# Post-norm attention and FFN layer on eight cores: WQ folds moved between the K/V chunks, and LayerNorm 1 moved into the attention loop

## The reference

```python
Q = x @ WQ.T + bQ                       # 2048 -> 16 heads of 128
K = (x @ WK.T + bK)  # 4 groups of 128  -> tiled 4 times to 2048 columns
V = (x @ WV.T + bV)  # the same
scores = einsum('btd,bsd->bts', Q, K)   # one score matrix over all 2048 columns
scores = where(causal, -inf, scores)
attn = softmax(scores) / sqrt(128)
x = layernorm(x + einsum('bts,bsd->btd', attn, V) @ proj)      # LayerNorm 1
g = (x @ gate_w.T) * gate_s ; u = (x @ up_w.T) * up_s
x = layernorm(x + ((silu(g) * u) @ down_w.T) * down_s)         # LayerNorm 2
```

## Time and profile before

| | us |
|---|---|
| median of two runs | 2189.18 (2187.82 to 2190.53) |
| the profiled execution | 2190.91 |
| its span on the slowest core (core 5) | 2189.3 |
| spans of the eight cores | 2161.7 to 2189.3 |
| TensorE busy | 1559.2 (71% of the span) |
| VectorE busy | 369.8 (17%) |
| ScalarE busy | 158.3 (7%) |
| gate and up matmuls (L698, L708) | 319.7 + 318.3 |
| down matmuls (L780) | 309.8 |

### The profile page before, as it was taken

How to read it: one execution, slowest core, us unless ns; L and a number is a source line. 1 busy time by engine, 2 the same in 40 slices (tenths; PEclk the granted TensorE clock), 3 DMA queues, 4 the chain that set the end, 5 groups by cost and what they waited for, 6 DMA issues and landing times. The chain is left out here.

```text
span 2189.3 us, 19673 instructions; the slowest of 8 cores (2161.7 to 2189.3 us)
## 1 busy us (share of the span) xinstructions
PE 1559.2 (71%) x7922; PEld 783.3 (36%) x7922; DVE 369.8 (17%) x510; ACT 158.3 (7%) x169; POOL 149.7 (7%) x143
## 2 busy tenths in 40 slices
PE   3269999645655556462009999999999969999930
PEld 0024443211212112120004444444444438888830
DVE  0000000014132232411600111111111110000035
ACT  1000000001000010100301111111111000000011
POOL 1100000010000000000001111111111100000000
PEclk9999999856565665655559999999999979999965
DMA  6955531370030300205495777777777784674466
GB/s 92 137 81 77 77 58 19 78 124 0 0 115 0 115 0 30 86 0 172 193 194 60 75 76 76 76 75 76 76 76 76 77 111 83 96 118 83 80 213 259
DMA packets 298527, 192.25 MB, mean 88 GB/s; under 512 B 201946, under 2 KB 284099, under 8 KB 291269
## 3 DMA queue, kind: packets, MB, share of 16 engines
q0 software_dynamic: 258240, 106.97, 41.4%
q1 hardware_dynamic: 40198, 84.02, 11.7%
HBM read 255.98 MB, written 37.75 MB: 134 GB/s over the span
## 5 line engine op out<-in xcount | busy, mean ns | idle before, releaser
L698 PE MATMUL gups<-x1T,gstr 128*128 128x512 bf16 x1408 | 319.7, 380 | 138.1 <-DMA x1T<-x1bd 138.1
L708 PE MATMUL gups<-x1T,ustr 128*128 128x512 bf16 x1408 | 318.3, 379 | 0.0
L780 PE MATMUL dnps<-dstr,hT 128*128 128x256 bf16 x2816 | 309.8, 274 | 10.3 <-DMA dstr<-dTd 10.3
L780 PEld LDWEIGHTS dnps<-dstr,hT 128*128 128x128 bf16 x2816 | 276.5, 98 | 45.0 <-issue 11.9
L698 PEld LDWEIGHTS gups<-x1T,gstr 128*128 128x128 bf16 x1408 | 138.1, 98 | 306.0 <-issue 140.9
L708 PEld LDWEIGHTS gups<-x1T,ustr 128*128 128x128 bf16 x1408 | 137.7, 98 | 166.2
L519 PE MATMUL zpn<-vv,aT_sb 128*128 128x512 bf16 x256 | 129.5, 609 | 79.4 <-DVE aT_sb L512 79.4
L723 DVE SCALAR_TENSOR_TENSOR hT<-gups,us_col,silu 128x512 bf16<-128x512 f32 x88 | 66.1, 751 | 592.4 <-PE gups L708 592.4
L314 PE MATMUL kps<-xch,wk_sb 128*128 128x512 bf16 x512 | 120.5, 390 | 44.2 <-DMA xch<-xT 42.0
L687 POOL DMA_DIRECT2D gstr<-gTd x44 | 50.3, 1144 | 1149.0 <-DMA x1bd<-x1s 625.1
L454 PE MATMUL scps<-kT,qsT 128*128 128x512 bf16 x256 | 78.7, 466 | 70.4 <-DVE scores L463 65.8
(11 more groups left out here) (96 smaller groups left out, 676.0 us busy)
## 6 DMA issues: line engine op xcount, KB each, us to landing
gstr<-gTd POOLq DMA_DIRECT2D x44, 512.0 KB, 7.7
ustr<-uTd POOLq DMA_DIRECT2D x44, 512.0 KB, 9.5
dstr<-dTd POOLq DMA_DIRECT2D x8, 2816.0 KB, 20.9
xch<-xT POOLq DMA_DIRECT2D x8, 2048.0 KB, 16.5
wq4b<-wq POOLq DMA_DIRECT2D x16, 512.0 KB, 6.5
masks<-msk SPq DMA_DIRECT2D x8, 1024.0 KB, 7.9
pjt<-prj POOLq DMA_DIRECT2D x16, 512.0 KB, 5.6
xqp<-xq SPq DMA_DIRECT2D x32, 256.0 KB, 5.9
```

The source lines that it names most:

```text
L698: (lambda bi, tch, gsl, ct: lambda e: e.matmul(gups[:, gsl, :], gstr[bi][:, ct, :], x1T[:, ct, tch*512:(tch+1)*512], start=(ct == 0), stop ...
L708: (lambda bi, tch, usl, ct: lambda e: e.matmul(gups[:, usl, :], ustr[bi][:, ct, :], x1T[:, ct, tch*512:(tch+1)*512], start=(ct == 0), stop ...
L780: (lambda bi, ts, ps, it: lambda e: e.matmul(dnps[ps][:, 0:256], hT[:, it, ts*128:(ts+1)*128], dstr[bi][:, it, :], start=(it == 0), stop=( ...
```

## The change

Three things are changed. The debug outputs are removed as well, which were not built.

First, in A1, the loads of the first x chunk, wk, the second x chunk and wv are issued first. The folds become a function, `plan_wq_fold`, that is called four times after the V product of each of the first four chunks. It accumulates in `kps` bank 0 instead of `vps` bank 0.

Second, in B, the body of the loop becomes three functions: `plan_scores`, `plan_z` (P times V with its transposes) and `plan_proj_ln1`. The projection of a group is planned after the scores of the next group and before its P times V. `plan_proj_ln1` also does LayerNorm 1 of each q tile in place, right after its four column blocks, and stores x1. Stage C, its DRAM tensor `y1d` and one barrier are gone. To make room, the proj rows are loaded into `Pq` instead of `pjtile`.

Third, the reciprocal root in both LayerNorms is Exp(-0.5 * Ln(var)) on ScalarE, instead of Sqrt on ScalarE and a reciprocal on VectorE.

```diff
+                    mx_pre[0] = B.dma("gpsimd",
...
+                                      "sxc0", [("pe", mp_a0), ("ve", mv_a0)])
+                    m_wk = B.dma("gpsimd", lambda e: e.dma_start(out=wk_sb[:], in_=wk_r),
+                                 "swkv")
+                    mx_pre[1] = B.dma("gpsimd",
...
+                                      "sxc1")
+                    m_wv = B.dma("gpsimd", lambda e: e.dma_start(out=wv_sb[:], in_=wv_r),
+                                 "swkv")
...
+                    def plan_wq_fold():
+                        dt_ = fold_dt[0]
+                        fold_dt[0] += 1
+                        fbi = dt_ % 2
+                        swq = "swq%d" % fbi
+                        mwq = B.dma("gpsimd",
...
+                                    swq, [("pe", wqf_free[fbi])])
+                        nonlocal_mk = mk_kfree_ref[0]
+                        for r in range(4):
+                            B.op("tensor",
+                                 (lambda fbi, r: lambda e: e.matmul(
+                                     kps[:, 0, :], idb_sb[:], wq4buf[fbi][:, r, :],
+                                     start=(r == 0), stop=(r == 3)))(fbi, r),
+                                 [(swq, mwq), ("ve", mv_a0), ("se", nonlocal_mk)]
+                                 if r == 0 else (),
...
+                        wqf_free[fbi] = B.m("pe")
+                        B.op("scalar",
...
+                        mk_kfree_ref[0] = B.m("se")
...
                     for pi, rc in enumerate(proc):
...
+                        if pi in mx_pre:
+                            mx = mx_pre[pi]
+                        else:
+                            mx = B.dma("gpsimd",
...
+                        if pi < 4:
+                            for _ in range(4):
+                                plan_wq_fold()
...
-                                 [("pe", mp_pj), (sxq, mxq), (sy, y1st[tq])],
+                                 [("pe", mp_pj), (sxq, mxq), (sx, slot_st[tq])],
...
+                        B.op("vector",
+                             (lambda q, tq: lambda e: e.tensor_reduce(
+                                 l1s[:, q:q+1], y1s[:, tq, :], axis=AX.X, op=OP.add))(q, tq),
+                             (), [("ve", 1)])
+                        B.op("scalar",
+                             (lambda q, tq: lambda e: e.activation(
+                                 out=sqscr[:], in_=y1s[:, tq, :], func=AF.Square,
+                                 accum_out=l1q[:, q:q+1]))(q, tq),
...
+                                 out=l1t[:, q:q+1], in_=l1v[:, q:q+1], func=AF.Ln))(q),
+                             [("ve", mv_var)], [("se", 1)])
...
+                                 out=l1r[:, q:q+1], in_=l1t[:, q:q+1], func=AF.Exp,
+                                 scale=-0.5))(q),
...
+                                 out=y1s[:, tq, :], in0=y1s[:, tq, :],
+                                 scalar1=l1nm[:, q:q+1], scalar2=l1r[:, q:q+1],
...
+                                 y1s16[:, tq, :], y1s[:, tq, :]))(tq),
...
+                                  out=x1f_r[q], in_=y1s[:, tq, :]))(q, tq),
+                              sx, [("ve", mv_a)])
...
+                                  out=x1b_r[q], in_=y1s16[:, tq, :]))(q, tq),
+                              sx)
+                        slot_st[tq] = B.m(sx)
...
+                pending = None
+                for g in range(4):
+                    plan_scores(g)
+                    if pending is not None:
+                        plan_proj_ln1(pending)
+                    plan_z(g)
+                    pending = g
+                plan_proj_ln1(pending)
```

More of the change, by code:

```diff
@@ L247, in build_program @@
                     B.begin()
-                    mvid = mv_a0
+                    proc = [2, 3, 4, 5, 6, 7, 0, 1]
+                    xuse = [0, 0]
+                    mk_kfree = 0
+                    mk_vfree = 0
                     wqf_free = [0, 0]
[L250 to L266, removed]
-                        wqf_free[bi] = B.m("pe")
-                        B.op("scalar",
-                             (lambda dt_: lambda e: e.activation(
-                                 out=wqsT[:, dt_, :], in_=vps[:, 0, :],
-                                 func=AF.Copy))(dt_),
-                             [("pe", wqf_free[bi])], [("se", 1)])
-                        mk_kfree = B.m("se")
@@ L438, in build_program, with plan_scores @@
                 pj_free = [mv_fold, mv_fold]
-                y1st = [0, 0]
                 xq_free = [0, 0]
                 zevac = 0
-                for g in range(4):
+                slot_st = [0, 0]
+                zT_used = 0
+                def plan_scores(g):
+                    nonlocal exp_prev
                     for q in (2 * g, 2 * g + 1):
@@ L534, in build_program @@
                                      zn_sb[:, tq, dv*128:(dv+1)*128], idb_sb[:]))(tq, dv),
[L535 removed]
+                                 [("ve", mv_zn), ("pe", zT_used)] if dv == 0 else (),
                                  [("pe", 1)] if dv == 3 else ())
@@ new lines, in plan_proj_ln1 @@
+                        B.op("vector",
+                             (lambda q: lambda e: e.tensor_scalar(
+                                 out=l1v[:, q:q+1], in0=l1v[:, q:q+1],
+                                 scalar1=float(EPS), scalar2=None, op0=OP.add))(q),
+                             (), [("ve", 1)])
+                        mv_var = B.m("ve")
+                        B.op("scalar",
+                             (lambda q: lambda e: e.activation(
+                                 out=l1t[:, q:q+1], in_=l1v[:, q:q+1], func=AF.Ln))(q),
+                             [("ve", mv_var)], [("se", 1)])
@@ L857, in build_program @@
             B.op("scalar", lambda e: e.activation(
-                out=tmp8[:], in_=var8[:], func=AF.Sqrt),
+                out=tmp8[:], in_=var8[:], func=AF.Ln),
                 [("ve", mv_v)], [("se", 1)])
+            B.op("scalar", lambda e: e.activation(
+                out=rstd8[:], in_=tmp8[:], func=AF.Exp, scale=-0.5),
+                (), [("se", 1)])
             ms_v = B.m("se")
-            B.op("vector", lambda e: e.reciprocal(rstd8[:], tmp8[:]),
-                 [("se", ms_v)], [("ve", 1)])
-            mv_r = B.m("ve")
             o_free = [0, 0]
```

207 lines of the change are left out of this document (82 added, 125 removed).

## The result

The changed kernel takes 2204.12 us (median of 18 runs), the kernel before 2196.37 us beside it (16 runs): a ratio of 1.0045, 95% interval 1.0032 to 1.0059. It is slower by 0.45%, far inside the 2% that I called no change; I had predicted 2197 us, within 2165 to 2232. That forecast stood on 2189.2 us for the kernel before, so it was 8 us more; 0.45% is 10 us more. The profiled execution's slowest core is core 3.

The account below looks back on a forecast made before the run. TensorE was taken as starved in the first 129 us and the 94 us between attention and FFN. Sum: 2190.9 + 39 (stage A) - 32 (B and C) = 2198, predicted as 2197 us, range 2165 to 2232.

Parts of the forecast that it names:

- the loads do not hide (1): Rival in A1: the x loads hide, all four fold blocks last 13.4 us, 35 us less, 2162; chance 0.15.
- not in 33 (2): Rival in A1: x chunk lands after 32.5 us, sharing engines with fold loads; 36 us more, 2233; chance 0.10.
- one in each stage with activations (3): Rival in LayerNorm: Ln and Exp need two table loads in each of eight, 20.5 us, 2217; chance 0.05.
- no step of P times V passes the LayerNorm (4): Rival in attention: P times V steps proceed while LayerNorm waits, saving up to 54 us, 2143; chance 0.03.
- (1): Start of A1: x, wk and wv loaded first, in at about 69 us (64 to 74), 60 us earlier.
- (2): A1, folds between chunks: two run at once, two wait for loads; next K starts at 13.4 us.
- (3): A1, GpSimd queue: x chunk waits behind fold loads at three places, 25 us each (20.8 to 29); blocks total 88.4.
- (4): A1: four more K rows start after waiting at the lower clock, 4 x 2.7 = 11.0 us, at least 0.
- A1 in sum: Stage A total: -60 + 88.4 + 11.0 = +39 us, between +15 and +56.
- (5): Attention, VectorE: P times V copies stand behind projection and LayerNorm 1 of two tiles, 42.5 us (38 to 48).
- (6): Attention: a pair takes 142.8 us; x1 transposes start at 1080.0 instead of 1111.9, gain 32 us (10 to 50).
- (7): Stage F: Ln and Exp for Sqrt and reciprocal cost 0; loading proj into Pq costs 0.

Follow-up runs that it names:

- e1: The kernel before with only phase A1 taken from the changed kernel: 2253.80 us, 1.0256 of the kernel before.
- e2: The changed kernel with phase A1 of the kernel before: 2148.00 us, 0.9767 of the kernel before.
- e3: The changed kernel with each x chunk's load issued one block earlier, behind its own block's fold loads: 2167.57 us, 0.9877 of the kernel before.
- e6: The changed kernel with LayerNorm 1 in pieces between steps of P times V, except the last pair's: 2152.79 us, 0.9764 of the kernel before.
- e9: The changed kernel with wv on its own semaphore and loaded ahead of the second x chunk: 2179.74 us, 0.9920 of the kernel before.
- e10: The changed kernel with the first two fold loads of blocks 1 to 3 held until their block's K is done: 2210.68 us, 1.0028 of the kernel before.
- e4: The kernel of e3 with six buffers for the fold loads instead of two: 2130.88 us, 0.9692 of the kernel before.

## Why the prediction was right, and where it was not

Right as mechanisms: the folds stand bare on TensorE; the x chunk waits for its turn in GpSimd's queue at three places; K restarts at the lower clock level; P times V stands behind LayerNorm 1; stage C's time comes back in the loop. The runs e1, e2, e3 and e6 each took one part away or alone, and each moved the time to the side that it should, e1 to e3 by about the amount, e6 by more (the gap between the tiles went with it). Of the rivals, none came: the loads do not hide (1), the x chunk lands in 20.0 to 25.8 us and not in 33 (2), the compiled kernel holds four table loads, one in each stage with activations (3), and no step of P times V passes the LayerNorm (4).

That 2197 us was so near is luck: A1 was forecast 17 us too cheap, B with C 26 us too dear (core 3), and the FFN's 7 us were not in the sum at all. The sizes, step by step, from the rows of core 3:

- (1) The first K at 73.3 us, predicted 69 (64 to 74). The 13 us a load in the lower bound stands on no row. What I took as given, that the first K must wait for wv, is what e9 shows to be worth 27 us.
- (2) Block 0: 15.0 us, predicted 13.4.
- (3) Blocks 1 to 3: 29.7, 30.5 and 27.4 us, 87.6 together, predicted 75. This is the mis-sized term of A1. I let 4 us count for the megabyte ahead of the x chunk. The rows of the changed kernel show that all of it is to be counted: the second of the two fold loads lands 8.7 to 9.7 us after its issue, and the chunk 13.9 to 17.8 us behind it, as long as a chunk takes alone (15.3 and 15.5 us); e10 rules out the loads behind. The upper bound that I had worked out, 29 us, was the right reading.
- (4) Cold K rows: 5.93, 5.15, 6.05 and 6.37 us, together 9.0 above 3.63, predicted 11.0. That the block itself takes the clock away was right: with blocks of 7.7 us (e4) the four rows take 3.6.
- A1 in sum: 4.3 + 1.6 + 12.6 - 2.0 is 16.5 more than the forecast +39, so 55.5; the table has 56.0.
- (5) The block on VectorE: 37.5 us, predicted 42.5. The copies of a tile take 6.0 us, not 8.0. I had taken 8.0 from the earlier trace rows, where the last copy of a tile waits 1.54 us for its load, here 0.25 and 0.45; the rest of why they were slower in the old order I did not test. LayerNorm itself took 8.8 us (predicted 9.0), the gap between the tiles 7.5 (8.4).
- (6) A pair: 136.7 us, predicted 142.8, on three pairs 18 us. The rest of the error is the last pair: 49.2 us from its zn cast to the transposes, predicted 55.0, and 2.0 us between the first mask load and the first zn cast, which I had left as they were.
- (7) Table loads and Ln with Exp: nothing, as predicted.
- The FFN was to stay as it was. The first down matmul waits 16.0 us for its weights on core 3, and waited 10.3 on core 5 before. In the kernel before, four cores began the gate matmuls some 17 us ahead of the other four and waited there 6.2 to 7.0 us, the later four 10.0 to 12.8; now all eight begin within 11 us of one another and wait 12.4 to 17.7. e1 and e2 place the longer wait in the new B: e1, with the old B, has the two groups of cores and waits of 6.3 to 14.1 us, e2, with the old A1, has all cores within 11 us and waits of 12.0 to 19.0. That the cores' loads slow one another is how I read it. I have not taken it away in an experiment, so the cause stays open.

The Trainium skill's formula for the cost of a load ("DMA: Bandwidth & Descriptors", Anatomy of one DMA), 2.0 us plus the bytes over 436 GB/s, gives an estimate of 6.8 us for 2 MB. No load of 2 MB in these runs landed in under 13.1 us after its issue, so the measurement decides.

## What to carry to other kernels

In this kernel a load's price was what stood ahead of it in its queue and its own transfer: count the bytes ahead in full, those behind not at all (e10), and ask what the queue's head waits for. Before work is moved into another engine's in-order row, look for the slack inside the steps of that row: LayerNorm as one piece ahead of P times V cost its whole length, 17.6 us a pair; the same instructions in pieces between its steps cost 1.2 to 1.9 us (e6). A result near zero can be two changes of 2.5% that undo each other: time each half alone, since keeping the good half (e2), or mending the bad one (e4), is worth more than either reading of the sum.

## What I had not expected of the hardware

- One semaphore for two loads made the first matmul 29 us later (73.5 us, in e9 44.1), though the first of the two loads had landed at 43.4 us (core 3).
- Four pauses of 0.9 us in a block of 7.7 us (e4) did not lower TensorE's clock level: the next sixteen matmuls took 3.61 us. In the changed kernel, whose blocks have pauses of up to 16 us, they took 4.9 to 6.5 us over the eight cores.
- Four fold loads instead of two at the start, 1 MB more in the same queue behind x, wk and wv, did not delay the first K (73.5 us in e4, 73.1 in e3).
- A 2 MB load with 1 MB ahead of it and 1 MB issued behind it while it was on its way landed no later than with nothing behind it (means of 22.0 to 23.1 us, in e10 22.6 to 23.6).
- On two cores of one die, in one execution (e10), sixteen matmuls took 4.37 us in nineteen or twenty rows each, in stretches whose granted clock reads 0.77 to 0.85; the same rows take 3.63 us elsewhere.
